# Another order of softmax, gather and sum steps in the attention stage of a fused attention and MoE kernel

## The chip, the cores and the metric

One core of one Trainium2 chip. The metric is the device time of one execution in microseconds (us): before the change a median of 512.95 us over 3 runs (512.67 to 513.08).

## The reference, cut to what matters

Four sequences of 1024 tokens with 256 features go through a layernorm, and then side by side through one attention head and a mixture of experts (16 experts, the best 2 of each token, and a shared one). The sum is added to the input. All is float32.

```
xn = layernorm(x)                                   # (4, 1024, 256)
q, k, v = xn@Wq.T+bq, xn@Wk.T+bk, xn@Wv.T+bv
p = softmax(q @ k.T / 16)                           # (4, 1024, 1024)
x = x + p @ v + moe(xn)                             # moe: top 2 of 16 experts + shared expert
```

## The kernel before, in words

The kernel has one list of named steps, made by `plan()` (lines 103 to 302). The five engine programs each walk through the same list and issue, for each step, their own part of it, so that the list fixes the order of work on every engine. Between engines there are semaphores only. Moving a step in the list therefore moves its part on TensorE (PE), VectorE (DVE), ScalarE (ACT), GpSimd (POOL) and SyncE (SP) together, but each only against the other steps that have a part on that engine.

The first part of the list is the layernorm, the router, the shared expert and the experts, which leave their results in the DRAM table `ytab`. The change touches only the part after it, a loop over `GROUPS` = 8 groups `g` of 512 queries (four tiles of 128, `CT` = 4), so that group `g` has the tiles n = 4g to 4g+3 (`new` to `new+3` in the code; `old` is 4g-4). Each matrix product is done in three passes over a high and a low part of the operands. The steps of the loop:

- `scores(g, pair)`, pair 0 to 3: PE computes two key tiles against the 512 queries (12 matmuls) into one of two pairs of PSUM banks. They are used in turn, also by `heads` and `values` (the ring, lines 840 to 852). ACT copies the pair to `scored_t` (`scores_copy`, line 1300). PE may write a bank pair again only when its copy is done: `scores(g, 2)` waits for the copy of `scores(g, 0)`. The copy of `scores(g, 0)` in turn waits until all four `less` steps of group g-1 have read `scored_t` (line 1309).
- `scores_max`: DVE takes the running maximum over the keys, per pair from pair 1 on. `tops`: DVE adds a shift and POOL takes the maximum over the partitions in two halves (`partition_all_reduce`, line 780), each followed by `spread` or `spread_second` on DVE (line 1664).
- For each tile n: `less` (DVE, line 1672) subtracts the maximum, `probs` (ACT, line 1319) takes the exponential, `probs_hi` (ACT, line 1325) copies the high part to `pT`, `probs_lo` (DVE, line 1678) the remainder. In the text below these are less(n), exp(n), hi(n) and lo(n). There are three buffers `probs_f`, so that less(n) waits for lo(n-3).
- `weigh(n)`: 24 matmuls of PE, `pT` times `v` (line 1118), which wait for lo(n). `weigh_sum(n)`: DVE divides by the row sum and adds to `acc` (lines 1694 and 1697), and SP stores the 128 rows of the output.
- `rows(i)`: DVE adds the two expert results of tile i to `acc` (line 1687, two instructions). With it goes the `gather` of tile i+3: two indirect DMAs of POOL from `ytab` (line 792), which wait for the two adds of tile i, since there are three buffers.
- `heads` and `values` (`ahead`, `behind`): the projections for later groups on PE, each with a split on ACT and DVE.

Of the kernel before, what the change touches and what calls it, by code (L numbers as in the profile page):

```python
# [30 lines left out]
GROUPS = NCH  # L31
# [71 lines left out]
def plan():  # L103


    steps, held = [], []
# [123 lines left out]
    def split(kind, b, u):  # L230
        return [(kind, b, u), (kind + "_split", b, u)]

    def scores(g, pair):
        return [("scores", g, pair), ("scores_copy", g, pair)]

    def weigh(n):
        return [("weigh", n), ("weigh_sum", n)]

    def rows(i):
        return [("rows_in", i), *([("gather", i + YR)] if i + YR < TILES else [])]  # L240

    def probs(n):
        return [("probs", n), ("probs_hi", n), ("probs_lo", n)]


    ahead = {1: split("heads", 1, 1), 2: split("heads", 2, 0), 3: split("heads", 2, 1), 4: split("heads", 3, 0),
             5: split("heads", 3, 1), 6: split("values", 3, 1)}
    behind = {2: split("values", 1, 1), 3: split("values", 2, 0), 4: split("values", 2, 1), 5: split("values", 3, 0)}
    def spread(g):
        return [("spread", g)]  # L250

    def spread_second(g):
        return [("spread_second", g), *([("shift_in", g + 2)] if g + 2 < GROUPS else [])]
# [2 lines left out]
    steps += [("gather", i) for i in range(YR)]  # L256
    for g in range(GROUPS):
        new, old = CT * g, CT * (g - 1)
        last = g == GROUPS - 1
        steps += scores(g, 0)  # L260
        if g == 1:
            steps += probs(new - 2)
        elif last:
            steps += [("probs_hi", new - 2), ("probs_lo", new - 2)]
        steps += scores(g, 1)
        if g == 1:
            steps += [("probs", new - 1), ("probs_hi", new - 1)]
        steps += [("scores_max", g, 1), *(rows(new) if g == 0 else [])]
        if g == 1:
            steps.append(("probs_lo", new - 1))  # L270
        if g:
            steps += weigh(old - 1 if last else old)
        steps += [*scores(g, 2), ("scores_max", g, 2), *(rows(new + 1) if g == 0 else [])]
        steps += [*scores(g, 3), ("scores_max", g, 3)]
        if g in (1, 3):
            steps.append(("keys_load", g // 2 + 2))
        if g == 0:
            steps += [*split("heads", 0, 1), ("heads", 1, 0), ("tops", g), ("heads_split", 1, 0),
                      ("values", 0, 1), *spread(g), ("values", 1, 0), ("less", new),
                      ("values_split", 0, 1), ("less", new + 1), *spread_second(g), ("probs", new), ("values_split", 1, 0),  # L280
                      ("less", new + 2), ("probs_hi", new), ("probs", new + 1), ("probs_hi", new + 1), ("probs_lo", new),
                      ("less", new + 3), ("probs_lo", new + 1), *rows(new + 2), *rows(new + 3)]
        elif not last:

            steps += [("tops", g), *ahead[g], *weigh(old + 1), *spread(g), ("less", new), ("probs", new), ("less", new + 1),
                      *spread_second(g), *behind.get(g, []), ("probs_hi", new), ("probs", new + 1), *rows(new),
                      *weigh(old + 2), ("probs_hi", new + 1), ("less", new + 2), ("probs_lo", new), *rows(new + 1),
                      ("probs", new + 2), ("less", new + 3), ("probs_lo", new + 1)]
            if g + 2 < GROUPS:
                steps += [("probs_hi", new + 2), *weigh(old + 3), ("probs", new + 3), ("probs_lo", new + 2), *rows(new + 2),  # L290
                          ("probs_hi", new + 3), ("probs_lo", new + 3), *rows(new + 3)]
            else:
                steps += [*rows(new + 2), *rows(new + 3), *rows(new + 4)]
        else:
            steps += [("tops", g), ("probs", new - 1), ("probs_hi", new - 1), *weigh(old), ("probs_lo", new - 1),
                      *weigh(old + 1), *spread(g), ("less", new), ("less", new + 1), *spread_second(g),
                      *[(kind, new + t) for t in range(2) for kind in ("probs", "probs_hi")], ("probs_lo", new),
                      ("less", new + 2), ("probs", new + 2), ("probs_hi", new + 2), ("less", new + 3),
                      ("probs", new + 3), ("probs_hi", new + 3), *weigh(old + 2), ("probs_lo", new + 1), *rows(new + 1),
                      *weigh(old + 3), ("probs_lo", new + 2), *rows(new + 2), ("probs_lo", new + 3), *rows(new + 3),  # L300
                      *sum((weigh(new + t) for t in range(CT)), [])]
    return steps

# [56 lines left out]

def build(nc, x, bv, Wqkv, bqk_in, Wr, We, Ws, const_f, const_b, out):
    steps = plan()
    places = Places(steps)
    nth, before = places.nth, places.before
# [1366 lines left out]
```

## Time and profile before

| | before |
|---|---|
| median of 3 runs | 512.95 us |
| profiled execution, its own time | 512.95 us |
| its span, first to last instruction | 511.1 us |
| PE busy / PE weight load busy | 503.8 / 462.0 us |
| DVE, ACT, POOL busy | 402.7, 279.5, 200.1 us |
| granted TensorE clock | 1.00 |

The span is cut by the page into 40 slices of 12.8 us. PE is at 90% or more in all of them but the first and the last, and the time outside the span is 1.85 us. Busy time of PE is modelled, since its matmuls overlap; a wait of PE stands in the profile as an idle time ahead of an instruction with the instruction that ended it.

### The profile page before, as it was taken

What the parts mean: (1) busy time and instruction counts of PE and PEld (TensorE: products, weight loads), DVE (VectorE), ACT (ScalarE), POOL (GpSimd) and SP (SyncE); (2) the same over time, 40 slices, a digit from 0 to 9 for tenths busy, and PEclk for the clock granted to TensorE, in tenths of its full rate; (3) what the DMA queues carried; (4) which work ended last, traced back from release to release, by engine and by line L of the source; (5) the groups of instructions that cost most, each with busy time, mean ns of one, the idle gap of its engine ahead of it and who ended that gap; (6) DMA issues with size and microseconds to landing.
All of it is one profiled execution on the core that took longest, in us unless ns stands there. A gap on an engine that the chain in (4) does not pass through costs nothing.

```text
span 511.1 us, 10075 instructions
## 1 busy us (share of the span) xinstructions
PE 503.8 (99%) x3410; PEld 462.0 (90%) x3411; DVE 402.7 (79%) x847; ACT 279.5 (55%) x466; POOL 200.1 (39%) x178
## 2 busy tenths in 40 slices
PE   8999999999999999999999999999999999999997
PEld 7898988888989999999999888989989898989986
DVE  5989457899997687777776389897969797888896
ACT  4787885246655464555555547464727364545641
POOL 0001021111005777777770451353554544362730
PEclk9999999999999999999999999999999999999999
DMA  8937176111113565786675730731262213131311
GB/s 311 410 117 280 82 294 233 50 45 39 56 63 114 176 195 182 235 291 195 196 142 148 253 120 25 218 97 53 84 203 98 60 62 84 42 92 32 94 43 63
DMA packets 31185, 71.28 MB, mean 139 GB/s; under 512 B 5312, under 2 KB 9792, under 8 KB 30112
## 3 DMA queue, kind: packets, MB, share of 16 engines
q1 hardware_dynamic: 23840, 51.80, 28.2%
q0 software_dynamic: 6864, 18.75, 14.3%
q8 instruction: 30, 0.49, 0.4%
q10 hardware_dynamic: 432, 0.09, 0.1%
q14 instruction: 19, 0.16, 0.1%
HBM read 43.34 MB, written 27.28 MB: 138 GB/s over the span
## 4 chain that ended last, share of the span: by engine, by line
PE 85%; DVE 7%; issue 4%; DMA 1%; POOL 1%; ACT 1%; POOLq 0%; DVEq 0%
PE ps L805 52%; PE ps L1015 10%; PE ps L945 7%; PE ps L811 6%; PE ps L1047 5%; PE ps L900 1%; PE ps L858 1%; DMA blk_x<-rows,row 1%; POOL rows_y L792 1%; DVE sil L1409 1%; DVE probs_f L1672 1%; PE ps L909 1%; DVE place_hot L1520 1%; DMA rows_y<-ytab,slot 1%; POOL blk_x L762 1%
## 5 line engine op out<-in xcount | busy, mean ns | idle before, releaser
L792 POOL DMA_INDIRECT rows_y<-ytab,slot x64 | 81.0, 1265 | 85.5 <-DVE acc L1687 67.4
L762 POOL DMA_INDIRECT blk_x<-rows,row x79 | 86.0, 1089 | 47.8 <-DVE row L1535 23.3
L805 PE MATMUL ps<-vv,pT 128*128 128x258 f32 x768 | 95.8, 283 | 2.1 <-DVE pT L1331 2.1
L805 PEld LDWEIGHTS ps<-vv,pT 128*128 128x128 f32 x768 | 94.7, 189 | 3.5 <-DVE pT L1331 2.5
L805 PE MATMUL ps<-xT,shared_w 128*128 128x512 f32 x384 | 92.6, 394 | 0.4 <-DVE sil L1409 0.3
L805 PEld LDWEIGHTS ps<-xT,shared_w 128*128 128x128 f32 x384 | 70.7, 188 | 15.5 <-issue 0.8
L805 PE MATMUL ps<-qT,xbT_hi 128*128 128x512 f32 x256 | 79.1, 390 | 0.0
L1015 PE MATMUL ps<-expert_w,blk_xT 128*128 x474 | 66.1, 288 | 0.4 <-DVE blk_xT L1331 0.4
L1015 PEld LDWEIGHTS ps<-expert_w,blk_xT 128*128 128x128 f32 x474 | 59.0, 190 | 0.6 <-issue 0.6
L1319 ACT ACTIVATE probs_f<-probs_f 128x1024 f32<-128x1024 f32 x32 | 33.8, 1056 | 42.6 <-DVE probs_f L1672 42.6
L1125 ACT ACTIVATE scored_t<-ps 128x1024 f32<-128x1024 f32 (+1 forms) x33 | 32.3, 996 | 43.7 <-PE ps L805 39.5
L805 PEld LDWEIGHTS ps<-qT,xbT_hi 128*128 128x128 f32 x256 | 47.0, 188 | 9.2
L746 POOL TENSOR_TENSOR expert_w<-stage_e,expert_w 128x768 fp32r<-128x768 f32 x7 | 13.4, 1911 | 105.8 <-ACT expert_w L1125 105.8
L805 PE MATMUL ps<-qT,xbT_lo 128*128 128x512 f32 x128 | 50.0, 390 | 0.0
L1331 DVE TENSOR_TENSOR blk_xT<-ps,blk_xT 128x512 fp32r<-128x512 f32 (+1 forms) x40 | 27.4, 684 | 20.8 <-ACT blk_xT L1125 20.6
L945 PE MATMUL ps<-shared_w,hT 128*128 128x256 f32 x336 | 42.8, 285 | 0.0
L945 PEld LDWEIGHTS ps<-shared_w,hT 128*128 128x128 f32 x336 | 41.2, 191 | 0.2
L1331 DVE TENSOR_TENSOR pT<-probs_f,pT 128x1024 fp32r<-128x1024 f32 x32 | 39.0, 1220 | 1.6 <-ACT pT L1125 1.6
L1672 DVE TENSOR_TENSOR probs_f<-scored_t,less_wide 128x1024 f32<-128x1024 f32 x32 | 38.4, 1220 | 0.4
L1047 PE MATMUL ps<-expert_w,blk_hT 128*128 x237 | 38.0, 296 | 0.0
L1125 ACT ACTIVATE pT<-probs_f 128x1024 fp32r<-128x1024 f32 x32 | 33.9, 1060 | 0.8
L1249 ACT ACTIVATE blk_sil<-ps 128x256 f32<-128x256 f32 (+1 forms) x40 | 15.2, 381 | 33.0 <-PE ps L1015 33.0
(166 smaller groups left out, 859.2 us busy)
## 6 DMA issues: line engine op xcount, KB each, us to landing
ytab<-blk_y SPq DMA_DIRECT2D x40, 256.0 KB, 2.7
keys<-xT SPq DMA_DIRECT2D x8, 1024.0 KB, 6.0
stage_e<-in_experts SPq DMA_DIRECT2D x16, 384.0 KB, 3.1
rows<-xn SPq DMA_DIRECT2D x8, 512.0 KB, 3.1
xbT_hi<-keys SPq DMA_DIRECT2D x8, 512.0 KB, 6.1
xbT_lo<-keys SPq DMA_DIRECT2D x8, 512.0 KB, 6.9
out<-acc SPq DMA_DIRECT2D x32, 128.0 KB, 1.7
acc<-in_x SPq DMA_DIRECT2D x7, 512.0 KB, 9.1
```

The costliest lines, as they stand in the source:

```text
L762: e.indirect_dma_start(out=blk_x[:, q, n, :], out_offset=None, in_=rows, in_offset=bass.IndirectOffsetOnAxis(ap=row[:, 2 * b + n:2 * b + n ...
L792: e.indirect_dma_start(out=rows_y[:, r, k, :], out_offset=None, in_=ytab, in_offset=bass.IndirectOffsetOnAxis(ap=slot[:, k, i:i + 1], axis=0),
L805: ins = e.matmul(dst, stationary(p, k), moving(q, k), start=(n == 0), stop=(n == total - 1))
L811: ins = e.transpose(dst[:, n * P:(n + 1) * P], s, ident)
L945: ins = e.matmul(ps[:, b, (n % 2) * D:(n % 2 + 1) * D], hT[:, p, j, n * P:(n + 1) * P], shared_w[:, q, 2 * KD * SH + j * D:2 * KD * SH + ( ...
L1015: ins = e.matmul(ps[:, 2 + r, n * D:(n + 1) * D], blk_xT[:, r, p, (n * KD + k) * P:(n * KD + k + 1) * P], weights(b, n, q, k * 2 * HID, 2 ...
L1047: ins = e.matmul(ps[:, 6 + r, n * D:(n + 1) * D], blk_hT[:, r, p, n * P:(n + 1) * P], weights(b, n, q, 2 * D, D), start=(at == 0), stop=(a ...
L1125: e.activation(hi, src, ACT.Copy).then_inc(done, 1)
L1249: e.activation(blk_sil[:, r, 0:used(b), :], gu[:, 0:used(b), 0:HID], ACT.Silu).then_inc(blk_silu, 1)
L1319: e.activation(probs_f[w][:, :, :], probs_f[w][:, :, :], ACT.Exp).then_inc(exp_made, 1)
L1331: e.tensor_tensor(lo, src, hi.bitcast(F32), ALU.subtract).then_inc(done, 1)
L1672: e.tensor_tensor(probs_f[w][:, :, :], scored_t[:, 0:KT, t * P:(t + 1) * P], less_wide[:, t * P:(t + 1) * P].unsqueeze(1).to_broadcast([P, ...
```

## The change

The function `plan()` alone is edited. Its effect on the loop:

- Groups 1 to 6: `tops` stands behind `weigh(old+1)` instead of ahead of `heads`, and `spread` with all that follows it stands behind `weigh(old+2)` instead of `weigh(old+1)`. The steps of the tiles are then grouped otherwise. For groups 1 to 5 all eight `probs` and `probs_hi` steps are still ahead of the next group's first copy.
- `rows(new)` and `rows(new+1)` stand earlier: behind `scores_max` of pairs 1 and 2 (group 1: pairs 2 and 3), where before they stood among the `less` and `probs_lo` steps.
- Group 7: `tops` stands behind `weigh(old)`, `less(new+2)` ahead of the first `probs_lo`, and `rows(28)`, which stood at the end of group 6, now stands behind `probs_lo(29)`; the other three follow later by one place.

```diff
-        last = g == GROUPS - 1
...
-        steps += [("scores_max", g, 1), *(rows(new) if g == 0 else [])]
+        late = g == GROUPS - 1
+        steps += [("scores_max", g, 1), *([] if late or g == 1 else rows(new))]
...
-            steps += weigh(old - 1 if last else old)
-        steps += [*scores(g, 2), ("scores_max", g, 2), *(rows(new + 1) if g == 0 else [])]
+            steps += weigh(old if g < GROUPS - 1 else old - 1)
+        steps += [*scores(g, 2), ("scores_max", g, 2), *([] if late else rows(new if g == 1 else new + 1))]
         steps += [*scores(g, 3), ("scores_max", g, 3)]
+        if g == 1:
+            steps += rows(new + 1)
...
-        elif not last:
-
-            steps += [("tops", g), *ahead[g], *weigh(old + 1), *spread(g), ("less", new), ("probs", new), ("less", new + 1),
-                      *spread_second(g), *behind.get(g, []), ("probs_hi", new), ("probs", new + 1), *rows(new),
-                      *weigh(old + 2), ("probs_hi", new + 1), ("less", new + 2), ("probs_lo", new), *rows(new + 1),
-                      ("probs", new + 2), ("less", new + 3), ("probs_lo", new + 1)]
+        elif g + 1 < GROUPS:
+            steps += [*ahead[g], *weigh(old + 1), ("tops", g), *behind.get(g, []), *weigh(old + 2),
+                      *spread(g), ("less", new), ("less", new + 1), *spread_second(g), ("less", new + 2), ("probs", new), ("probs_hi", new),
+                      ("probs", new + 1), ("probs_hi", new + 1), ("probs", new + 2),
+                      *([("probs_hi", new + 2)] if g + 2 < GROUPS else []), ("probs_lo", new), ("less", new + 3),
+                      *(weigh(old + 3) if g + 2 < GROUPS else []), ("probs_lo", new + 1),
+                      *rows(new + 2), *([("probs_lo", new + 2)] if g + 2 < GROUPS else []), *rows(new + 3)]
             if g + 2 < GROUPS:
-                steps += [("probs_hi", new + 2), *weigh(old + 3), ("probs", new + 3), ("probs_lo", new + 2), *rows(new + 2),
-                          ("probs_hi", new + 3), ("probs_lo", new + 3), *rows(new + 3)]
-            else:
-                steps += [*rows(new + 2), *rows(new + 3), *rows(new + 4)]
+                steps += probs(new + 3)
         else:
-            steps += [("tops", g), ("probs", new - 1), ("probs_hi", new - 1), *weigh(old), ("probs_lo", new - 1),
-                      *weigh(old + 1), *spread(g), ("less", new), ("less", new + 1), *spread_second(g),
-                      *[(kind, new + t) for t in range(2) for kind in ("probs", "probs_hi")], ("probs_lo", new),
-                      ("less", new + 2), ("probs", new + 2), ("probs_hi", new + 2), ("less", new + 3),
-                      ("probs", new + 3), ("probs_hi", new + 3), *weigh(old + 2), ("probs_lo", new + 1), *rows(new + 1),
-                      *weigh(old + 3), ("probs_lo", new + 2), *rows(new + 2), ("probs_lo", new + 3), *rows(new + 3),
+            steps += [("probs", new - 1), ("probs_hi", new - 1), *weigh(old), ("tops", g), ("probs_lo", new - 1),
+                      *weigh(old + 1), *spread(g), ("less", new), ("less", new + 1), *spread_second(g), ("less", new + 2),
+                      *[(kind, new + t) for t in range(3) for kind in ("probs", "probs_hi")], ("probs_lo", new),
+                      ("less", new + 3), ("probs", new + 3), ("probs_hi", new + 3), *weigh(old + 2), ("probs_lo", new + 1), *rows(new),
+                      *weigh(old + 3), ("probs_lo", new + 2), *rows(new + 1), ("probs_lo", new + 3), *rows(new + 2),
+                      *rows(new + 3),
                       *sum((weigh(new + t) for t in range(CT)), [])]
```

## Rows read from the trace of the kernel before

**Rows 1.** Busy time by engine, windows view: start:end, length, busy us (instructions).
```profile
core 0: us, PE busy (x) PEld busy (x) DVE busy (x) ACT busy (x) POOL busy (x), PEclk, DMA share, GB/s
364.00:392.00 28.00, 28.00 (x182) 25.65 (x181) 23.18 (x35) 14.44 (x15) 13.46 (x11) 1.00 0.43 141
494.00:511.10 17.10, 12.23 (x98) 11.66 (x96) 12.99 (x24) 6.20 (x7) 0.00 (x0) 1.00 0.14 47
```
**Rows 2.** The last weigh products on PE, timeline: start us, us, instruction, idle before.
```profile
474.11 3.07 PE L805 MATMUL ps<-vv,pT 128*128 128x258 f32 x24
...
482.50 11.67 PE L805 MATMUL ps<-vv,pT 128*128 128x258 f32 x96
495.38 3.16 PE L805 MATMUL ps<-vv,pT 128*128 128x258 f32 x24 [1.22 <-DVE pT L1331]
499.38 8.91 PE L805 MATMUL ps<-vv,pT 128*128 128x258 f32 x72 [0.84 <-DVE pT L1331]
```
**Rows 3.** PE timeline, groups 1 to 3.
```profile
325.21 8.81 PE L805 MATMUL ps<-vv,pT 128*128 128x258 f32 x72
342.25 0.63 PE L805 MATMUL ps<-qT,xbT_hi 128*128 128x512 f32 x2
353.35 0.40 PE L805 MATMUL ps<-w_v,xbT_hi 128*128 128x256 f32 x2
362.00 0.63 PE L805 MATMUL ps<-qT,xbT_hi 128*128 128x512 f32 x2
367.49 3.02 PE L805 MATMUL ps<-vv,pT 128*128 128x258 f32 x24
370.35 0.62 PE L805 MATMUL ps<-qT,xbT_hi 128*128 128x512 f32 x2
```
**Rows 4.** DVE timeline behind weigh(old+1) of group 2.
```profile
353.55 0.17 DVE L1694 RECIPROCAL rsum<-ps 128x1 f32<-128x1 f32 x1 [0.50 <-PE ps L805]
354.61 2.36 DVE L1672 TENSOR_TENSOR probs_f<-scored_t,less_wide 128x1024 f32<-128x1024 f32 x2
356.88 0.42 DVE L1664 TENSOR_TENSOR less_wide<-shift_wide,top_keys 128x256 f32<-128x256 f32 x1
```
**Rows 5.** ACT timeline: first exponential of group 2; later passes of group 1.
```profile
355.87 1.06 ACT L1319 ACTIVATE probs_f<-probs_f 128x1024 f32<-128x1024 f32 x1 [4.53 <-DVE probs_f L1672]
...
331.72 1.06 ACT L1125 ACTIVATE pT<-probs_f 128x1024 fp32r<-128x1024 f32 x1
332.69 1.05 ACT L1319 ACTIVATE probs_f<-probs_f 128x1024 f32<-128x1024 f32 x1
333.76 1.06 ACT L1125 ACTIVATE pT<-probs_f 128x1024 fp32r<-128x1024 f32 x1
339.03 1.06 ACT L1125 ACTIVATE pT<-probs_f 128x1024 fp32r<-128x1024 f32 x1
339.99 1.92 ACT L1125 ACTIVATE scored_t<-ps 128x1024 f32<-128x1024 f32 x2
```
**Rows 6.** DVE timeline, groups 1 and 2.
```profile
322.58 2.55 DVE L1647 TENSOR_TENSOR top_keys<-top_keys,scored_t 128x1024 f32<-128x1024 f32 x2
359.01 1.00 DVE L1687 SCALAR_TENSOR_TENSOR acc<-rows_y,score,acc 128x256 f32<-128x256 f32 x2
```
**Rows 7.** POOL timeline: first gathers, then an all-reduce, then the four gathers of group 2.
```profile
289.13 1.01 POOL L792 DMA_INDIRECT rows_y<-ytab,slot  x1 [0.30 <-issue]
326.75 2.11 POOL L780 PARTITION_ALL_REDUCE top_keys<-top_keys  x2 [3.80 <-DVE top_keys L1656]
360.78 1.87 POOL L792 DMA_INDIRECT rows_y<-ytab,slot  x1 [6.84 <-DVE acc L1687]
362.96 1.20 POOL L792 DMA_INDIRECT rows_y<-ytab,slot  x1 [0.30 <-issue]
364.57 1.25 POOL L792 DMA_INDIRECT rows_y<-ytab,slot  x1 [0.41 <-issue]
366.12 1.01 POOL L792 DMA_INDIRECT rows_y<-ytab,slot  x1 [0.30 <-issue]
```
**Rows 8.** Expert rows: the tile view's summary, whole span.
```profile
L792 POOL DMA_INDIRECT rows_y<-ytab,slot x64: 1007/1198/2038, 287.8 to 486.0; - x64
DMA to landing us min/median/max: 2.7/3.1/6.2
```
**Rows 9.** PE and DVE timeline, groups 6 and 7 to the end.
```profile
462.84 5.95 PE L805 MATMUL ps<-vv,pT 128*128 128x258 f32 x48
477.01 0.63 PE L805 MATMUL ps<-qT,xbT_hi 128*128 128x512 f32 x2
508.53 0.48 DVE L1697 SCALAR_TENSOR_TENSOR acc<-ps,rsum,acc 128x256 f32<-128x256 f32 x1
```

More of the change, by code:

```diff
@@ L262, in plan @@
             steps += probs(new - 2)
-        elif last:
+        elif g == GROUPS - 1:
             steps += [("probs_hi", new - 2), ("probs_lo", new - 2)]
```

## The prediction

> **What bounds the kernel now.** I read the windows by engine first, then the waits of PE, then the timelines of PE, ACT, DVE and POOL over one group. In groups 1 to 6 PE is busy for the whole of each stretch, DVE for 23 of 28 us, ACT and POOL for half or less [rows 1]. The only idle time of PE in the loop is in the last four tiles: 1.22 us ahead of weigh(28) and 0.84 us ahead of weigh(29), both ended by a `probs_lo` of DVE [rows 2]. So no order of steps can win much more than these 2.06 us and a little of DVE's end, while every wait that a new order gives PE is paid in full. The first question is whether PE's own order changes. Reading both lists for PE alone (scores, heads, values, weigh), it does not: in every group the same products come in the same sequence. What changes is when ACT, DVE and POOL deliver, against a PE that has no slack of its own.
>
> **The period of a group on PE.** From rows 3: weigh(1) to weigh(3) take 325.21 to 333.85, where the products of the next group follow at once, so 2.88 us each. In group 2 weigh(old+2) ends at 362.00 - 2.88 = 359.12. From there come weigh(old+3), 2.88, scores 0 and 1 of the next group, 362.00 to 367.49, 5.49, and weigh(new), 2.86, and scores(g+1, 2) starts at 370.35. That is 11.23 us.
>
> **Groups 1 to 5: the copy that PE waits for.** scores(g+1, 2) writes the banks of scores(g+1, 0), so it needs their copy by ACT, and that copy stands behind four exponentials and four high copies of group g in ACT's queue, before and after the change.
> - Before, exp(new) starts 2.52 us after the end of weigh(old+1): PE goes on at 353.35, DVE has the row sum at 353.55, less(new) at 354.61, and ACT starts at 355.87 [rows 3 to 5]. The copies of scores(3, 0) and (3, 1) then begin at about 367.0 and PE needs the first at 370.35, so there were some 2.3 us to spare.
> - After, `spread` and less(new) stand behind weigh_sum(old+2). DVE executes in order, so the same 2.52 us now count from the end of weigh(old+2), which is one `weigh` and, in groups 2 to 5, one `values` later: 359.12 - 353.35 = 5.77 us.
> - From the first exponential ACT is without a gap, since DVE's less steps come every 1.14 to 1.25 us, and the last one, behind lo(new), ends about 5.1 us after exp(new) starts, a microsecond before its exponential is due. By rows 5 an exponential and its copy start 1.07 to 1.09 us apart (one waits for the other) and the next exponential 0.97 later: 331.72 to 333.76 is 2.04, and I take 2.06. The last high copy is followed by the scores copy 0.96 later. Four pairs: 3 x 2.06 + 1.09 + 0.96 = 8.23 us. The copy itself takes 1.01 (1.92 for two), and PE starts about 0.05 after what releases it.
> - Chain: 2.52 + 8.23 + 1.01 + 0.05 = 11.81 us, against 11.23 of PE work. PE waits 0.58 us, and behind a wait 24 matmuls take 3.16 us, where undisturbed ones take 3.07 [rows 2], so 0.09 more. Loss 0.67 per group. There is no catching up, because the next group's chain starts again from PE's own weigh.
> - The terms rest on one microsecond in twelve, so I bound the loss of a group: 0.3 (pairs of 2.00 and no refill) to 0.9 (each link 0.03 longer).
> - Four groups lose just this (scores(3,2), (4,2), (5,2) and (6,2)): 4 x 0.67 = 2.68 us.
>
> What else could be late there: lo(new) ends 3.8 us after exp(new), 6.3 after weigh(old+2), and weigh(new) wants it after 8.4, so it is not. The `rows` steps have moved; their gathers are issued three tiles ahead, with POOL free about 5 us before `tops` is needed. SP keeps the order of its stores, and `shift_in` is wanted two groups later.
>
> **Group 1: POOL is late too.** Here no `values` stands between weigh(1) and weigh(2), and rows(4) and rows(5) now come ahead of `tops` with their gathers. POOL's queue then holds gather(7), gather(8), then the all-reduce. rows(4) follows the first of the two maxima at 322.58 and ends at about 324.7; POOL starts 0.77 after such an end (359.01 + 1.00 to 360.78) [rows 6, 7], at 325.5. Four gather instructions take 6.35 us (360.78 to 366.12 + 1.01), until 331.8; with a gap of 0.30 and half of the all-reduce's 2.11, the first half is there at 333.2. DVE would have been ready for it at 330.97 + 0.20 + 0.61 = 331.8. So exp(4) is 1.4 us later still, and the loss at scores(2, 2) (342.25 in rows 3) is 0.53 + 1.43 + 0.09 = 2.05 us (here the PE work is 342.25 - 330.97 = 11.28). Bounds: with POOL in time 0.6; with four gathers of the longest duration, 2.04 [rows 8], 4.7.
>
> A gather on POOL takes 1.01 us while DVE rests (289.13) and up to 1.87 while it works [rows 7]. The Trainium skill (GPSIMD Engine Reference, section 8, Key points) says that GpSimd shares its SBUF interfaces with VectorE and contends with DVE instructions that read two SBUF inputs; the adds and maxima that stand beside gather(7) and gather(8) are of that kind, and the rows agree. If it held them up nowhere, four would take 4 x 1.01 + 3 x 0.30 = 4.94 and with the wait for rows(5) the group would lose about 0.9 instead of 2.05.
>
> **Group 6 to 7.** Only five ACT passes stand ahead of the copy of scores(7, 0), but there is no weigh(old+3) on PE either: scores(7, 2) starts at 477.01, 8.39 after weigh(22) (462.84 + 2 x 2.89 = 468.62) [rows 9]. Chain: 2.52 + 2 x 2.06 + 0.96, at which point the last less has just ended too, + 1.01 + 0.05 = 8.66. Loss 0.27 + 0.09 = 0.36 us.
>
> **Group 7 and the end, on the clock of before.** `tops` now waits for weigh_sum(24): PE ends that at 482.50 + 0.36 + 2.88 = 485.7, so `tops` ends at 487.2 instead of 487.9, and weigh(25), ending at 488.6, then sets exp(28) at 491.15 (before 491.9). less(30) stands ahead of lo(28), which ends 3.83 later, at 494.98: weigh(28) starts at 495.03 against 495.38. less(31), weigh_sum(26) and lo(29) follow, until 497.98, and weigh(29) starts at 495.03 + 2.98 = 498.01 against 499.38 [rows 2]. PE's last product would end at 506.7. But rows(28) ends only at 498.9, and its gather is that of tile 31: 0.77 + 1.87 + 0.30 + 3.05 to landing [rows 7, 8] is 504.9. Then rows(31), three weigh_sums at 0.60 and the last of 0.68: 504.9 + 0.92 + 1.80 + 0.68 = 508.3, against 509.01 (508.53 + 0.48) [rows 9]. So this part gains 0.73 us, its own loss of 0.36 included. Bounds: a gain of 1.4, if the gather lands in time, to a loss of 2.4, if it lands after 6.2.
>
> **Sum.** 2.05 + 2.68 - 0.73 = +4.0 us. The profiled execution took 512.95 us, as the median did: 516.9 us.
>
> **Rivals.**
> - *The copy is early after all and the end wins.* If a filled ACT queue ran its dependent passes every 0.96 us as it does independent ones, the eight would take 7.7 instead of 8.23, the chain 11.28, and groups 2 to 5 would lose nothing; group 7 then gains 0.73 + 0.36 = 1.1 us. It decides at a chain of 11.23. With gathers as short as 1.01 group 1 would cost 0.3: 512.95 + 0.3 - 1.1 = 512.1 us; with POOL late, 513.2. Against it speak the 1.07 to 1.09 in every pair, also where ACT had been behind [rows 5]. 8%.
> - *POOL is in time in group 1.* The forecast without the 1.43: 515.5 us. For it: 289.13 and 1.01. Against: every gather pair close behind a DVE add begins with 1.87. 14%.
> - *Gathers cost more.* They are slow in group 1, while the keys of sequence 2 load, up to 2.6 us more, or that of tile 31 lands after 6.2 instead of 3.05 us, 3.1 more: about 519.8 us. For it: the ranges in rows 8. Against: the medians there, 1.20 and 3.1. 8%.
> - *The forecast*, 516.9 us, own range 515.0 to 518.2: 70%.
>
> **How the numbers follow.** Less than 0.2% (1.0 us) can't be told from no change. Faster: half of the first rival and its like, 0.04. Same: the rest of it and small losses, 0.06. Slower 0.90. The range reaches from 514.4, losses of 0.3 per group with POOL half in time, to 518.7, losses of 0.9.
>
> **What would show it.** PE's timeline: new idle times of 0.5 to 0.7 us ahead of scores(3,2), (4,2), (5,2) and (6,2), ended by ACT's scores copy, one of about 2 us ahead of scores(2,2) and one of 0.3 ahead of scores(7,2); the wait ahead of weigh(28) halved and that ahead of weigh(29) gone; ACT from exp(new) to the copy without a gap; DVE waiting for the all-reduce in group 1 and for the gather of tile 31 at the end; a group's period of 28.7 instead of 28.0 us. I am wrong if PE shows none of the idle times in the middle, or if another wait of DVE holds a `probs_lo`.

## The result, and the profile after

The changed kernel takes 516.86 us in the median of four runs (516.21 to 518.26), the kernel before 512.92 in runs beside them (512.67 to 513.08). The ratio is 1.0076, with a 95% interval of 1.0063 to 1.0089: slower by 3.9 us. The prediction was 516.9. The sum came out, but two of its terms were wrong, by 0.94 and 0.84 us, in opposite directions.

The first profiled execution of the changed kernel is of no use for a sum. Its span is 535.1 us, 20 us of it ahead of the loop, where the change touches nothing: from 175 to 185 us PE's granted clock there is 0.66. No timed run is that long. In the loop it has the same six waits as below (0.96, 0.35, 0.41, 0.36, 0.30 and 0.30 us). All rows below are from a second profile of the same kernel, the first experiment ("again"): span 516.4, own time 518.15 us. All its lines are two further down than before (L807 for L805, L1127 for L1125, and so on).

PE's waits, longest sums first (engine, tile, line, what it waited for: us in total, times, longest):

```profile
PE ps L807 <- ACT scored_t L1127: 2.7, 6, 0.9
PE ps L860 <- DVE xT L1335: 1.5, 1, 1.5
PE ps L1017 <- DVE blk_xT L1333: 1.0, 1, 1.0
PE ps L807 <- DVE pT L1333: 0.8, 1, 0.8
```

The first row is new, and nothing of the kind stood there before. The last was 2.1 us in two waits [rows 2]. The two between belong to the stages ahead of the loop. PE's timeline, the places where it waited in the loop, and weigh(1) ahead of them (start, us, instruction, count, idle time before and its releaser):

```profile
326.44 8.81 PE L807 MATMUL ps<-vv,pT 128*128 128x258 f32 x72
...
344.59 0.73 PE L807 MATMUL ps<-qT,xbT_hi 128*128 128x512 f32 x2 [0.95 <-ACT scored_t L1127]
...
373.29 0.74 PE L807 MATMUL ps<-qT,xbT_hi 128*128 128x512 f32 x2 [0.34 <-ACT scored_t L1127]
...
401.99 0.73 PE L807 MATMUL ps<-qT,xbT_hi 128*128 128x512 f32 x2 [0.40 <-ACT scored_t L1127]
...
430.66 0.73 PE L807 MATMUL ps<-qT,xbT_hi 128*128 128x512 f32 x2 [0.36 <-ACT scored_t L1127]
...
459.37 0.72 PE L807 MATMUL ps<-qT,xbT_hi 128*128 128x512 f32 x2 [0.31 <-ACT scored_t L1127]
...
482.46 0.73 PE L807 MATMUL ps<-qT,xbT_hi 128*128 128x512 f32 x2 [0.30 <-ACT scored_t L1127]
...
500.51 11.94 PE L807 MATMUL ps<-vv,pT 128*128 128x258 f32 x96 [0.80 <-DVE pT L1333]
```

These are the six places that the prediction named: ahead of scores(2,2), (3,2), (4,2), (5,2), (6,2) and (7,2). Read the starts, not the idle times: the loop's period is 28.70, 28.70, 28.67 and 28.71 us, while scores(6,2) stood at 454.49 before, 112.24 behind the 342.25 of [rows 3], or 28.06 per group:

```profile
454.49 0.63 PE L805 MATMUL ps<-qT,xbT_hi 128*128 128x512 f32 x2
```

So a group loses 0.64 us where the bracket shows 0.35. Of the rest, about 0.1 lies behind the wait (0.73 for the first two matmuls instead of 0.63 [rows 3]) and 0.16 ahead of it: the 24 matmuls of weigh are shown with 3.02 us, but where nothing waits the next product starts 2.86 after their start (367.49 to 370.35 [rows 3]).

At the end, the wait ahead of weigh(28) fell from 1.22 to 0.80, and the one ahead of weigh(29) is gone: 96 products in one stretch where there were 24 and 72 [rows 2].

The whole account, as differences of starts in the two traces:

| stretch | before | after | lost | predicted |
|---|---|---|---|---|
| start to weigh(1), which the change doesn't touch | 325.21 | 326.44 | 1.23 | 0 |
| weigh(1) to scores(2,2) | 17.04 | 18.15 | 1.11 | 2.05 |
| scores(2,2) to scores(6,2), four groups | 112.24 | 114.78 | 2.54 | 2.68 |
| scores(6,2) to scores(7,2) | 22.52 | 23.09 | 0.57 | 0.36 |
| scores(7,2) to the end of DVE's last instruction | 32.00 | 31.75 | -0.25 | -1.09 |

Without the first row, 3.97 us are lost, and the medians say 3.94. The first row is no part of the effect: in the ten variants below weigh(1) started anywhere from 324.68 to 327.04, and weigh(0), which stands ahead of every step that was moved, starts 11.1 us before it in both traces. That is a spread among executions in the stages ahead, and it is why the experiments below are compared by medians and by differences within the loop.

### The profile page after: what moved, and what is told of

Its sections match the earlier page's. It is cut to its first block, busy times and chain, and to the rows that moved or that the text cites. A ratio compares the mean times of both kernels' runs of the same rounds, so it can differ in the third digit from the quotient of the medians.

```text
span 535.1 us, 10076 instructions
## 1 busy us (share of the span) xinstructions
PE 515.9 (96%) x3411; PEld 466.1 (87%) x3411; DVE 402.2 (75%) x847; ACT 277.3 (52%) x466; POOL 194.9 (36%) x178
## 4 chain that ended last, share of the span: by engine, by line
PE 69%; DVE 12%; ACT 8%; issue 8%; POOL 1%; DMA 1%; another core or an unknown queue 0%; POOLq 0%; DVEq 0%; ACTq 0%
PE ps L807 37%; PE ps L1017 10%; PE ps L813 7%; PE ps L947 6%; PE ps L1049 6%; ACT probs_f L1321 4%; DVE probs_f L1674 3%; ACT scored_t L1127 2%; PE ps L902 1%; POOL rows_y L794 1%; PE ps L964 1%; DVE blk_h L1571 1%; ACT blk_sil L1251 1%; DVE pT L1333 1%; DVE less_wide L1666 1%
## 5 line engine op out<-in xcount | busy, mean ns | idle before, releaser
L764 POOL DMA_INDIRECT blk_x<-rows,row x79 | 81.4, 1030 | 71.5 <-PE ps L813 26.1
L807 PEld LDWEIGHTS ps<-vv,pT 128*128 128x128 f32 x768 | 94.6, 189 | 2.1 <-DVE pT L1333 1.0
L807 PE MATMUL ps<-vv,pT 128*128 128x258 f32 x768 | 95.7, 283 | 0.8 <-DVE pT L1333 0.8
L807 PE MATMUL ps<-xT,shared_w 128*128 128x512 f32 x384 | 92.6, 394 | 0.4 <-DVE sil L1411 0.3
L807 PEld LDWEIGHTS ps<-xT,shared_w 128*128 128x128 f32 x384 | 70.7, 188 | 15.5 <-issue 0.9
L807 PE MATMUL ps<-qT,xbT_hi 128*128 128x512 f32 x256 | 79.8, 393 | 2.7 <-ACT scored_t L1127 2.7
L1017 PE MATMUL ps<-expert_w,blk_xT 128*128 x474 | 67.6, 293 | 1.0 <-issue 1.0
L1017 PEld LDWEIGHTS ps<-expert_w,blk_xT 128*128 128x128 f32 x474 | 60.4, 193 | 2.7 <-issue 2.4
L807 PEld LDWEIGHTS ps<-qT,xbT_hi 128*128 128x128 f32 x256 | 47.0, 188 | 13.1 <-ACT scored_t L1127 3.9
L807 PE MATMUL ps<-qT,xbT_lo 128*128 128x512 f32 x128 | 49.9, 390 | 0.0
L1127 ACT ACTIVATE scored_t<-ps 128x1024 f32<-128x1024 f32 (+1 forms) x33 | 32.4, 996 | 31.7 <-PE ps L807 27.9
L1571 DVE TENSOR_TENSOR blk_h<-blk_sil,ps 128x256 f32<-128x256 f32 (+1 forms) x40 | 16.5, 413 | 40.1 <-ACT blk_sil L1251 37.5
L1049 PE MATMUL ps<-expert_w,blk_hT 128*128 x237 | 39.8, 304 | 1.1 <-issue 1.1
L1049 PEld LDWEIGHTS ps<-expert_w,blk_hT 128*128 128x128 f32 x237 | 32.1, 195 | 4.1 <-issue 3.9
```

The source lines that it names most:

```text
L764: e.indirect_dma_start(out=blk_x[:, q, n, :], out_offset=None, in_=rows, in_offset=bass.IndirectOffsetOnAxis(ap=row[:, 2 * b + n:2 * b + n ...
L807: ins = e.matmul(dst, stationary(p, k), moving(q, k), start=(n == 0), stop=(n == total - 1))
L1017: ins = e.matmul(ps[:, 2 + r, n * D:(n + 1) * D], blk_xT[:, r, p, (n * KD + k) * P:(n * KD + k + 1) * P], weights(b, n, q, k * 2 * HID, 2 ...
L1049: ins = e.matmul(ps[:, 6 + r, n * D:(n + 1) * D], blk_hT[:, r, p, n * P:(n + 1) * P], weights(b, n, q, 2 * D, D), start=(at == 0), stop=(a ...
L1127: e.activation(hi, src, ACT.Copy).then_inc(done, 1)
L1571: e.tensor_tensor(blk_h[:, r, 0:used(b), :], blk_sil[:, r, 0:used(b), :], gu[:, 0:used(b), HID:2 * HID], ALU.mult).then_inc(blk_hidden, 1)
```

## The experiments

**The chain, seen again.** The changed kernel itself, for a second profile and more timed runs.

> The changed kernel itself, once more, beside the three variants of this batch. Its first trace shows PE idle ahead of scores(g,2) in groups 2 to 7 (0.96, 0.35, 0.41, 0.36, 0.30, 0.30 us, ended by ACT's scores copy) and 0.81 us ahead of weigh(28). Expected 516.3 to 517.3 us, and the same idle times within 0.1 us, with a span near 515 us.

Measured: 516.84 us (516.34 to 518.15), ratio 1.0073 (1.0052 to 1.0093). ACT's timeline in group 2 of it:

```profile
364.04 1.06 ACT L1321 ACTIVATE probs_f<-probs_f 128x1024 f32<-128x1024 f32 x1 [4.16 <-DVE probs_f L1674]
365.14 1.06 ACT L1127 ACTIVATE pT<-probs_f 128x1024 fp32r<-128x1024 f32 x1
366.11 1.04 ACT L1321 ACTIVATE probs_f<-probs_f 128x1024 f32<-128x1024 f32 x1
...
371.27 1.06 ACT L1127 ACTIVATE pT<-probs_f 128x1024 fp32r<-128x1024 f32 x1
372.23 1.92 ACT L1127 ACTIVATE scored_t<-ps 128x1024 f32<-128x1024 f32 x2
```

From the first exponential to the copy are 8.19 us, eight passes without a gap. The first of the two copies is done 1.01 later, at 373.24, and PE starts at 373.29. The prediction had 8.23, 1.01 and 0.05. The first link, from the end of weigh(6) (358.66 + 2.88 = 361.54) to the first exponential, is 2.50 where it had 2.52.

**The copy put ahead of the last pair.** If the eight passes ahead of the copy are the cause, six must be enough to free PE. The products, and PE's order, stay as they are.

```
         steps += scores(g, 0)
+        if 2 <= g < GROUPS - 1:
+            steps += probs(new - 1)
...
-            if g + 2 < GROUPS:
-                steps += probs(new + 3)
```

> The changed kernel with one move: in groups 1 to 5 the three steps probs, probs_hi, probs_lo of tile new+3 stand behind scores(g+1,0) and its copy. On PE, DVE, POOL and SP the order stays as it was; on ACT alone the copy of scores(g+1,0) comes ahead of exp(new+3) and hi(new+3). Theory (PE waits for the copy because eight ACT passes stand ahead of it): the chain gets 2.04 us shorter, the waits ahead of scores(2,2) to (6,2) go, and with them 1.12 + 4 x 0.65 = 3.7 us: 513.1 us, leaving the wait ahead of scores(7,2). Rival (PE is held by later probs_lo steps or by the all-reduce that comes later, and the copy is only the record nearest to it): DVE and POOL are unchanged, so the time stays at 516 to 517 us.

Measured: 513.1 us (512.42 to 514.7), ratio 1.0002 (0.9981 to 1.0023). Of the loss of 4.09 us, by the medians of this round (516.84 and 512.75), 3.74 are gone. In the traces, from weigh(1) to DVE's last instruction, the kernel before takes 183.80 us, the changed one 187.77 and this one 184.14. ACT's timeline in group 2, from the third high copy, and PE's waits in the whole loop:

```profile
366.31 1.06 ACT L1127 ACTIVATE pT<-probs_f 128x1024 fp32r<-128x1024 f32 x1
367.28 1.01 ACT L1127 ACTIVATE scored_t<-ps 128x1024 f32<-128x1024 f32 x1
368.19 1.04 ACT L1321 ACTIVATE probs_f<-probs_f 128x1024 f32<-128x1024 f32 x1
```
```profile
PE ps L807 <- DVE pT L1333: 0.8, 1, 0.8
...
PE ps L807 <- ACT scored_t L1127: 0.3, 1, 0.3
```

The copy begins 6.15 us after the first exponential (361.13), and of six waits for it one is left, that of scores(7,2), which this edit does not touch. In this kernel POOL's queue in group 1 is as it was in the changed one. So POOL's lateness alone costs nothing: it acts only through the copy.

**The start moved forward instead.** `spread` and the first two `less` go back ahead of weigh(old+2) in groups 1 to 5, and the eight passes stay ahead of the copy.

```
-            steps += [*ahead[g], *weigh(old + 1), ("tops", g), *behind.get(g, []), *weigh(old + 2),
-                      *spread(g), ("less", new), ("less", new + 1), *spread_second(g), ...
+            steps += [*ahead[g], *weigh(old + 1), ("tops", g), *behind.get(g, []), *([] if g + 2 < GROUPS else weigh(old + 2)),
+                      *spread(g), ("less", new), ("less", new + 1), *(weigh(old + 2) if g + 2 < GROUPS else []), *spread_second(g), ...
```

> The changed kernel, but in groups 1 to 5 spread, less(new) and less(new+1) stand ahead of weigh(old+2) instead of behind it; tops stays where the change put it, and on ACT the copy still has eight passes ahead of it. On DVE they then wait for the all-reduce and, in groups 2 to 5, for the remainder of values, which ends about 5.3 us after weigh(old+1), where the row sum of weigh(old+2) came at 6.0 and was done at 6.6: exp(new) starts 1.3 us earlier. Theory (only the length of the chain from its start to the copy matters): the waits ahead of scores(3,2) to (6,2) go, 4 x 0.66 = 2.6 us less than the changed kernel; in group 1 the start hangs on POOL and its wait of 0.95 us stays: 514.2 us. Rival (eight passes ahead of the copy are too many wherever they start): 516.8 us.

Measured: 514.28 us (513.79 to 515.43), ratio 1.0026 (1.0014 to 1.0037): 1.43 us over the kernel before beside it, so about 2.6 us of the loss are gone. ACT in group 2, and PE's first wait in the loop:

```profile
361.41 1.06 ACT L1321 ACTIVATE probs_f<-probs_f 128x1024 f32<-128x1024 f32 x1 [2.88 <-DVE probs_f L1674]
...
369.60 1.92 ACT L1127 ACTIVATE scored_t<-ps 128x1024 f32<-128x1024 f32 x2
```
```profile
343.23 0.73 PE L807 MATMUL ps<-qT,xbT_hi 128*128 128x512 f32 x2 [0.95 <-ACT scored_t L1127]
```

The chain is as long as in the changed kernel, 8.19 us, and only starts earlier, by 1.27 us as counted from scores(2,2); the waits ahead of scores(3,2) to (6,2) are gone. That of group 1 is left as it was: there DVE now waits 1.97 us for POOL's all-reduce, and `less_wide`, the first step of the chain, starts as late as in the changed kernel, 6.77 us after weigh(1). So this run measures the term of four groups by itself. In the traces, from scores(2,2) to scores(7,2), it takes 135.32 us and the changed kernel 137.87: 2.55 us where the prediction had 2.68.

**The chain made longer.** Three exponentials of one column each on ACT behind the last high copy of groups 1 to 5, with an output that nothing reads.

```
-                steps += probs(new + 3)
+                steps += [*probs(new + 3), ("pad", g)]
```

> The changed kernel with three exponentials of one column more on ACT in groups 1 to 5, between probs_hi(new+3) and the copy of scores(g+1,0); they write a scratch column that nothing reads. In the profile of before such an ACTIVATE takes 0.20 us and the next starts 0.15 us after it, so 0.45 to 0.6 us more in the chain. Theory (PE waits for the end of ACT's chain, with no slack left): each wait grows by that whole amount, 5 x 0.45 to 5 x 0.6 = 2.3 to 3.0 us more than the changed kernel: 519.1 to 519.8 us. Rival (the chain had slack, or another wait runs beside it): less than 1 us more.

Measured: 518.4 us (517.73 to 520.11), ratio 1.0105 (1.009 to 1.012). ACT and then PE in group 2:

```profile
372.13 1.06 ACT L1128 ACTIVATE pT<-probs_f 128x1024 fp32r<-128x1024 f32 x1
373.09 0.37 ACT L1326 ACTIVATE pad_out<-zero 128x1 f32<-128x1 f32 x3
373.37 1.92 ACT L1128 ACTIVATE scored_t<-ps 128x1024 f32<-128x1024 f32 x2
```
```profile
374.43 0.73 PE L808 MATMUL ps<-qT,xbT_hi 128*128 128x512 f32 x2 [0.62 <-ACT scored_t L1128]
```

The expectation overpriced the three: they delay the copy by 0.28 us (1.24 behind the last high copy, where it was 0.96), not by 0.45 or more. Each of the five waits grew by just that, 0.27 or 0.28 (0.34 to 0.62 here, 0.95 to 1.22 ahead of scores(2,2)). Five times 0.27 are 1.35; the traces, from weigh(1) to the end, differ by 1.37, and the medians, of two rounds, by 1.56. The point that it was to test holds: what is added to the chain is paid in full, because PE has no other slack.

**POOL's part in group 1.** rows(5), with gather(8), put behind `tops`, so that two gathers and not four stand ahead of the all-reduce.

```
-        if g == 1:
-            steps += rows(new + 1)
...
-            steps += [*ahead[g], *weigh(old + 1), ("tops", g), *behind.get(g, []), *weigh(old + 2),
+            steps += [*ahead[g], *weigh(old + 1), ("tops", g), *(rows(new + 1) if g == 1 else []), *behind.get(g, []), ...
```

> The changed kernel with rows(5) and gather(8) moved behind tops in group 1. Theory: in group 1 POOL's gathers stand ahead of the all-reduce and delay exp(4); in the first trace of the changed kernel exp(4) starts 0.5 us later than PE's weigh(2) asks for, so 0.5 us less: 516.4 us, with the wait ahead of scores(2,2) down from 0.96 to about 0.5 us. By the prediction's own sum it would be 1.4 us less: 515.4. Rival (POOL is in time anyway): no change, within 0.2 us.

Measured: 516.28 us (515.44 to 519.85), ratio 1.0067 (1.0042 to 1.0092). PE at scores(2,2):

```profile
342.75 0.73 PE L805 MATMUL ps<-qT,xbT_hi 128*128 128x512 f32 x2 [0.34 <-ACT scored_t L1125]
```

The wait is 0.34 instead of 0.95, the size that it has in every other group, and weigh(1) to scores(2,2) takes 17.53 instead of 18.15. POOL's lateness was worth 0.6 us in the trace and 0.56 in the medians, not the 1.43 of the prediction. Intervals of this width don't show the 0.56 by themselves; it is the trace that does. `less_wide` starts 0.19 us sooner here, as counted from weigh(1), and takes 0.42 us instead of 0.84: together the whole 0.61.

**The middle and the end apart.** One kernel has groups 1 to 6 as changed and group 7 as before, the other the reverse; rows(28) stands each time where the version of group 7 has it. The edits swap the branches of `plan()` that the diff shows. First the middle alone:

> Groups 1 to 6 as changed, group 7 as before (rows(28) at the end of group 6). In the trace of the changed kernel scores(7,2) starts 4.2 us later than before, counted from scores(1,3), and the rest from there took 32.0 us before. Theory (the loss is all in the middle, the new end is worth only 0.2 to 0.3 us): 512.75 + 4.2 = 516.9 us, as slow as the full change. Rival (the prediction's sum, in which the end gives back 1.1 us from scores(7,2) on): this kernel would be about 1 us slower than the full change, 517.9 us.

Measured: 517.18 us (516.85 to 517.69), ratio 1.0089 (1.0074 to 1.0103). Its waits ahead of weigh(28) and weigh(29) are 0.84 us each, and from scores(7,2) (481.17) to the end (512.90) are 31.73 us, as in the changed kernel (31.75): when scores(7,2) is late, the old order of group 7 gives back as much as the new one. Then the end alone:

> Groups 1 to 6 as before, group 7 as changed (rows(28) behind probs_lo(29)). Theory: the weigh products get earlier (weigh(28) 0.4, weigh(29) 1.4 us), but the end hangs on gather(31), so 0.2 to 0.4 us are left: 512.75 - 0.3 = 512.4 us, with a DVE wait for the gather of 1.7 us. The prediction's sum has 1.1 us here: 511.7 us.

Measured: 512.54 us (511.94 to 513.2), ratio 0.9996 (0.9987 to 1.0005). By the medians the new order of group 7 gains about 0.3 us in either company. In the traces it gains 0.26 with the old middle (31.74 us from scores(7,2) to the end, for 32.00) and nothing with the new one (31.75 for 31.73), and the interval here leaves room for no gain at all. DVE's timeline near its end:

```profile
502.56 1.00 DVE L1687 SCALAR_TENSOR_TENSOR acc<-rows_y,score,acc 128x256 f32<-128x256 f32 x2
505.34 1.01 DVE L1687 SCALAR_TENSOR_TENSOR acc<-rows_y,score,acc 128x256 f32<-128x256 f32 x2 [1.79 <-DMA rows_y<-ytab,slot]
```

DVE stands 1.79 us in front of rows(31), waiting for the gather that rows(28) issued too late.

**rows(28) put back to the end of group 6.** In the changed kernel, then in the kernel before with the new group 7:

```
             if g + 2 < GROUPS:
                 steps += probs(new + 3)
+            else:
+                steps += rows(new + 4)
...
-                      ... ("probs_lo", new + 1), *rows(new),
-                      *weigh(old + 3), ("probs_lo", new + 2), *rows(new + 1), ("probs_lo", new + 3), *rows(new + 2), *rows(new + 3),
+                      ... ("probs_lo", new + 1), *rows(new + 1),
+                      *weigh(old + 3), ("probs_lo", new + 2), *rows(new + 2), ("probs_lo", new + 3), *rows(new + 3),
```

> The changed kernel with rows(28) and with it gather(31) back at the end of group 6, the other rows of group 7 one place earlier as before the change. Theory (the end is set by the landing of gather(31), which rows(31) waits for): the end comes at PE's last product, 0.9 us earlier: 515.9 us, no wait of DVE for the gather in the last 10 us. But the two adds of rows(28) then run ahead of DVE's lo(26) and of the last maxima and can push tops(7) later, by at most 0.9 us. Rival (the end is set by PE's last product, the gather lands beside it): within 0.2 us.

Measured: 516.16 us (515.53 to 517.79), ratio 1.0062 (1.004 to 1.0084), 0.7 us under the changed kernel. DVE's last rows:

```profile
512.63 0.17 DVE L1697 RECIPROCAL rsum<-ps 128x1 f32<-128x1 f32 x1 [1.61 <-PE ps L808]
512.84 0.48 DVE L1700 SCALAR_TENSOR_TENSOR acc<-ps,rsum,acc 128x256 f32<-128x256 f32 x1
```

Now DVE waits for PE at the end, as it did before (1.60), and from scores(7,2) (482.27) to the end are 31.05 us: a gain of 0.95 on the 32.00. The gather was what ate the end's gain. In the changed kernel this place is harmless: DVE adds the rows of three tiles at a stretch there, from 482.15 to 484.98, and waits for no gather.

> As the last one, but with rows(28) and gather(31) at the end of group 6 as before the change: a candidate for a version better than both. The changed kernel with this same move takes 31.05 us from scores(7,2) to DVE's last instruction, where before took 32.00. Theory: 512.75 - 0.95 = 511.8 us, without a wait for the gather, ended by PE's last product. Rival (the adds of rows(28) and the wait for their gather push tops(7) as they did before): 512.5 us.

Measured: 514.01 us, ratio 1.0012 (0.9998 to 1.0026), the median of twelve runs in two clusters that differ in TensorE's mean granted clock: six from 512.30 to 513.69 us with 1.000 and six from 514.33 to 515.02 with 0.997. Theory and rival both expected less (511.8 and 512.5), and both were wrong. PE's row of weigh(28) to (31), and the windows around its start (start:end, length, busy us of PE, PEld, DVE, ACT and POOL, granted clock, DMA share, GB/s), of a profiled execution of the second cluster, with 514.64 us:

```profile
496.77 13.21 PE L804 MATMUL ps<-vv,pT 128*128 128x258 f32 x96 [2.23 <-DVE pT L1330]
```
```profile
494.50:496.77 2.27, 0.04 (x1) 0.00 (x0) 2.22 (x2) 2.24 (x3) 0.00 (x0) 0.97 0.00 0
496.77:499.00 2.23, 2.23 (x10) 2.23 (x11) 2.14 (x4) 2.20 (x3) 0.00 (x0) 0.50 0.00 0
499.00:501.00 2.00, 2.00 (x15) 2.00 (x14) 1.93 (x5) 1.97 (x3) 0.00 (x0) 0.74 0.19 66
501.00:503.00 2.00, 2.00 (x20) 2.00 (x19) 1.96 (x4) 0.14 (x1) 0.00 (x0) 1.00 0.24 74
```
```profile
480.14 1.00 DVE L1686 SCALAR_TENSOR_TENSOR acc<-rows_y,score,acc 128x256 f32<-128x256 f32 x2 [1.30 <-DMA rows_y<-ytab,slot]
```

The last fence is DVE at rows(28): it waited 1.30 us for its own gather, and all behind it in DVE's order, the maxima and `tops` of group 7, came later (`tops` at 487.97, where the end alone has 486.14; 0.39 of the difference stem from the stages ahead). So weigh(28) waited 2.23 us. And then came a second price: PE took 13.21 us for the 96 products, where the other kernels that have them in one stretch take 11.94 to 11.98. The granted clock stood at 0.50, the level of 1.2 GHz, with 10 matmuls in 2.23 us, then at 0.74 in the mean of 2 us, and only then at 1.00. The first cluster, whose mean clock is 1.000, seems to have been spared it, though no trace of one of its runs was taken; the medians of the two differ by 1.7 us.

**rows(28) where its gather has landed and nothing urgent is behind it.** Groups 1 to 6 as before and the new group 7, with rows(28) behind weigh(23), then with rows(28) behind `tops(7)`:

```
             steps += weigh(old - 1 if last else old)
+        if last:
+            steps += rows(new)
...
-                steps += [*rows(new + 2), *rows(new + 3), *rows(new + 4)]
+                steps += [*rows(new + 2), *rows(new + 3)]
```

> Groups 1 to 6 as before, group 7 as changed, but rows(28) behind weigh(23), ahead of the last two maxima. The last attempt of this kind had rows(28) in group 6, where DVE waited 1.30 us for its gather, tops(7) came 1.8 us later, PE was idle 2.23 us ahead of weigh(28) and then had a granted clock of 0.50. Here the gather of tile 28 has landed by then, and DVE has 0.77 us to spare ahead of tops. Theory: gather(31) lands before the end, which comes at PE's last product: 0.7 to 0.9 us less than the version with rows(28) behind probs_lo(29) (512.54): 511.8 us. Rival (gather(31) now stands ahead of POOL's last all-reduce and delays it by more than that gains): 512.5 us or more.

> As the last one with rows(28) behind tops(7) and ahead of probs_lo(27), so that the last all-reduce is ahead of gather(31) on POOL. Theory: DVE has 0.47 us to spare here, the two adds take 0.92, so weigh_sum(25) and with it weigh(28) come 0.4 us later, while the end no longer waits for the gather: 0.7 us less than 512.54: 511.8 us. Rival (every delay of exp(28) is paid at the end): 512.9 us.

Measured: 511.56 us (511.11 to 512.69), ratio 0.9971 (0.996 to 0.9983), and 511.62 (511.28 to 512.54), ratio 0.9969 (0.9958 to 0.998). Both beat the kernel before by 0.3%. PE's row of weigh(28), then two rows of DVE, of the first:

```profile
494.54 11.97 PE L806 MATMUL ps<-vv,pT 128*128 128x258 f32 x96 [0.90 <-DVE pT L1332]
```
```profile
480.73 1.00 DVE L1688 SCALAR_TENSOR_TENSOR acc<-rows_y,score,acc 128x256 f32<-128x256 f32 x2
...
506.55 0.17 DVE L1695 RECIPROCAL rsum<-ps 128x1 f32<-128x1 f32 x1 [1.59 <-PE ps L806]
```

No wait ahead of rows(28), none for the gather of tile 31, and 30.75 us from scores(7,2) (476.48) to the end (507.23): a gain of 1.25 on the 32.00. The second has 30.90 there. So the new order of group 7 held a gain, once rows(28) is taken out of it.

## Why the prediction came out as it did

- **What bounds the kernel.** Right. PE had no slack in the loop, and the added ACT passes were paid at a slope of one.
- **The chain of groups 2 to 5.** Right, link by link: 2.50 for 2.52, 8.19 for 8.23, 1.01 and 0.05 as read, so 11.75 for 11.81, and 2.54 us between the starts and 2.55 by experiment for 2.68. Only the sign to look for came out smaller: the prediction named idle times of 0.5 to 0.7 us (and of 2 in group 1), and the profile shows 0.31 to 0.40 (and 0.95), since it hides a part of what a wait costs. This rested on the 1.07 to 1.09 us between an exponential and its own copy [rows 5]. The rival that let ACT run its passes every 0.96 falls by the same rows of after: 1.10, 0.97, 1.07, 0.97.
- **Group 1.** The place and the cause were right, the size was not: 1.11 us for 2.05. The mis-sized term is POOL's 1.43, for which the runs show 0.61. I took 6.35 us for four gathers, from the four of [rows 7], and held against shorter ones that every pair close behind a DVE add begins with 1.87. The trace of before does not say so: of its twelve series of gathers that a DVE add released after an idle time of POOL, six begin with 1.87 and six with 1.06 to 1.48, and the four gathers from 317.52 on take 5.43 us:

```profile
317.52 1.06 POOL L792 DMA_INDIRECT rows_y<-ytab,slot  x1 [12.73 <-DVE acc L1687]
...
342.45 1.25 POOL L792 DMA_INDIRECT rows_y<-ytab,slot  x1 [2.35 <-DVE acc L1687]
```

  POOL's timeline in the changed kernel, and DVE's `less_wide` behind it:

```profile
326.71 1.25 POOL L794 DMA_INDIRECT rows_y<-ytab,slot  x1 [2.54 <-DVE acc L1689]
328.27 1.01 POOL L794 DMA_INDIRECT rows_y<-ytab,slot  x1 [0.30 <-issue]
329.58 1.01 POOL L794 DMA_INDIRECT rows_y<-ytab,slot  x1 [0.30 <-issue]
330.90 1.22 POOL L794 DMA_INDIRECT rows_y<-ytab,slot  x1 [0.30 <-issue]
332.16 2.06 POOL L782 PARTITION_ALL_REDUCE top_keys<-top_keys  x2
```
```profile
332.62 0.48 DVE L1699 SCALAR_TENSOR_TENSOR acc<-ps,rsum,acc 128x256 f32<-128x256 f32 x1
333.21 0.84 DVE L1666 TENSOR_TENSOR less_wide<-shift_wide,top_keys 128x256 f32<-128x256 f32 x1
```

  The four take 5.41 us with their gaps, near the 4.94 that the prediction worked out for gathers that nothing holds up. So "POOL is in time" was nearer for this term, with nothing for 0.61, and wrong about the total, since its sum (515.5) kept the gain at the end. What was left, 0.2 us of wait for the first half of the all-reduce, had a companion that the prediction lacked: `less_wide` took 0.84 us instead of 0.42 [rows 4], because it now runs beside POOL's all-reduce. That this is the reason is an inference from where it happens. The same step took 0.73 to 0.84 beside the all-reduce of group 7 in most kernels, and 0.42 in group 1 of the run with rows(5) put back, where the all-reduce was all but over (POOL's record ends 0.18 us behind its start). But in three kernels (before, the middle alone, rows(28) behind `tops`) it took 0.41 or 0.42 in group 7 as well, although POOL's record ends only as it does (490.61 and 490.62 before); there the all-reduce had been the slower one, with 2.56 to 3.10 us for 2.11. What decides which of the two is held up stays open. The Trainium skill (GPSIMD Engine Reference, section 8, Key points) says that GpSimd and VectorE contend for SBUF when a DVE instruction reads two SBUF inputs. The 0.84 agrees with it, as seen from DVE's side. For the four gathers here, which run in part beside DVE's two-input adds and maxima, it can be worth no more than 0.47 us (5.41 for 4.94), not the 1.41 that the prediction charged.
- **scores(7,2).** 0.57 for 0.36. From exp(24) at 476.12 to the copy at 481.38 are 5.26 us where I had 5.08. The link that was longer is DVE's: the copy also waits for less(27), which ends at 481.28, so it starts 1.16 behind exp(26) (480.22) and not 0.96.
- **The end.** The step that was off is "so this part gains 0.73", which is 1.09 from scores(7,2) on; the trace has 0.25. That the gather of tile 31 would set the end was right, and also that PE would no longer. DVE's rows at the end:

```profile
494.60 0.73 DVE L1666 TENSOR_TENSOR less_wide<-shift_wide,top_keys 128x256 f32<-128x256 f32 x1
...
503.43 1.00 DVE L1689 SCALAR_TENSOR_TENSOR acc<-rows_y,score,acc 128x256 f32<-128x256 f32 x2
...
510.84 1.00 DVE L1689 SCALAR_TENSOR_TENSOR acc<-rows_y,score,acc 128x256 f32<-128x256 f32 x2 [1.72 <-DMA rows_y<-ytab,slot]
...
513.73 0.48 DVE L1699 SCALAR_TENSOR_TENSOR acc<-ps,rsum,acc 128x256 f32<-128x256 f32 x1
```

  On the clock of before, moved by the 5.09 us between scores(7,2) here (482.46) and as predicted (477.01 + 0.36), rows(28) was to end at 504.0 and ended at 504.4. Its gather was to be there 3.05 us after its second issue (507.37) and DVE went on 3.47 after it. The 0.44 and the 0.42 are the missing 0.8. Of the first, 0.31 are `less_wide` again, 0.73 for 0.42. And the middle alone shows that even the 0.25 are not the new order's merit: beside the new middle the old group 7 gives them back too.
- **The cancellation.** That the total fits is luck: the prediction lost 0.94 us too much in group 1 and gained 0.84 too much at the end, and the 0.1 us left met 0.07 of the opposite sign from the groups between (0.14 too much) and scores(7,2) (0.21 too little). A total that comes out right by 0.04 us does not show that its terms are right; the differences of starts and the kernels that hold one piece each do.

Open: why the first gather behind a DVE add takes 1.25 us in one place and 1.87 in another; what lengthens the stages ahead of the loop in single executions, by up to 2.4 us and once by 20.

## What to carry to other kernels

Where one engine has no slack, lay the other engines' queues beside it as a chain (what starts it, how many passes, what it ends in) and compare it with the work that the full engine has in that time: here 11.8 against 11.2 us decided the result, and moving the one copy that the full engine needs ahead of two passes that it does not need yet won nearly everything back. A step that also issues a transfer (here the adding of rows, which frees the buffer of a gather) has a latest place, set by the landing, and an earliest one, set by its own operand; each was missed by one of these versions, and the two kernels that put it between them are the fastest of this study. Read the loss off the starts in the two timelines, since here the idle time shown was only half of it.

## What the runs showed of the hardware

- In one trace (rows(28) at the end of group 6, before the new group 7), after 2.23 us without a product PE's granted clock was 0.50 for the next 2.23 us and 0.74 in the mean of the 2 us after that, and 96 products took 1.26 us longer (13.21 for 11.95). Six of the twelve runs of that kernel have the lower mean clock, six have not. After waits of 1.09 and 0.80 us they took 11.98 and 11.94, and before the change 1.22 us cost weigh(28) no more than 0.84 cost another one (3.16 us, as in the middle alone; 3.07 without a wait [rows 2]). The wait of 2.23 us thus cost half as much again as it shows.
- A DVE `tensor_tensor` of 128x256, 0.42 us by itself, took 0.73 to 0.84 in most places where it started beside a partition all-reduce of POOL. That all-reduce took 2.56 to 3.10 us in group 7, where DVE had two-input passes beside it, and 2.06 to 2.13 in most other places.
- An ACTIVATE of 128x1 added 0.09 us to ACT's queue; the three took 0.28 together.
